# Attention phase of a decoder layer: the key scores of every unit alternate with the projections

## The chip, the core and the metric

One core of a Trainium2 chip runs the whole program. It has five engines that work side by side, each through its own queue in order: TensorE (PE, matrix products; its loading of weights is shown as PEld), VectorE (DVE), ScalarE (ACT), GpSimd (POOL) and SyncE (SP), which issues the transfers. Engines wait for each other by semaphores only, so an instruction that waits also holds up everything behind it on its own engine. The metric is the time of one execution on the device in microseconds (us); lower is better.

## What is computed

Three sublayers follow each other over x of shape 8 x 512 x 512, each with a residual sum and a layer norm. Only the first, the self-attention, is touched by the change. Cut to what matters:

```python
kv = _ln(x, kvn_w, kvn_b) @ kv_w + kv_b            # 8 x 512 x 1024
q  = _ln(x, qn_w, qn_b) @ q_w + q_b
q, k = _rotary(q, ...), _rotary(k, ...)            # 16 heads of 32
qn, kn = _ln(q, ln_w, ln_b), _ln(k, ln_w, ln_b)    # over a head's 32
scores = einsum('bhqd,bhkd->bhqk', qn, kn) / sqrt(32)
attn = softmax(scores, axis=-1)
a = einsum('bhqk,bhkd->bhqd', attn, v)
x = _layernorm(x + (a @ out_w + out_b))            # then retention and the coupling network
```

## The kernel before, in words

The attention works in **units**: one batch entry b of 8 and one group g of four heads (G = 4, HG = 4), so 32 units, U = 4 b + g. A matrix with 512 rows has four tiles of 128 (T = K = 4), so a unit has T x HG = 16 score tiles of 128 x 512. Each engine's function `unit` goes through 16 **steps** i = 0 to 15, and tables at the head of the file say how many items of each kind have been issued by the end of a step; `within(DONE, i)` gives those that belong to step i. Three units are under way at once on PE. In unit U it issues

- the **query scores** of unit U + 1 (`query_scores`, product at L912, table QS_DONE: none in steps 0 and 1, then one or two a step until step 13). They only serve the softmax: DVE takes the maximum of each row (`row_max`, L527), ACT exponentiates and sums in place (`sum_exps`, L776, one step later). They go through three PSUM banks, so query score m waits for the sum of m - 3.
- the **key scores** of unit U (`key_scores`, L932, table KS_DONE), the same scores with keys on the partitions and the maximum taken off. ACT turns each into probabilities (`exps`, L797). They go through two banks: key score m waits for the exponential of m - 2.
- the **projections** for unit U + 3 (`project_item`, table PROJECT_DONE, sixteen items, each of the three products L887, L888 and L889; four items make one tile of q, k and v), which DVE saves (`save_qkv`, L490 and L492, SAVE_AFTER). Items of the third and fourth tile wait until an earlier tile is saved; with g = 0 there is one bank for them, and each new tile waits for the last one.
- the **weighing** (`weigh`, L942, table WEIGH_AT): four times a unit, the probabilities of one tile of keys times v, for all four heads. It waits for the exponentials of its tile; the exponentials of the tile after the next wait for it, since there are two sets of `probs`.
- two turns of normalised heads (`turn_item`, L898, TURN_AT), the turned inverses of the sums (`spread_inverse`, L950, step 11) and the turned maxima (`transpose_max`, L919, step 14).

Between two units lies one chain: all row maxima, `transpose_max` on PE, `save_max` on ACT (L789, two copies), `spread_max` on DVE (L533). Key scores 0 and 1 wait for one copy each, key score 2 for `spread_max`. The text below calls the start of `save_max` **S**; the time from one S to the next is the length of a unit. At the start of a unit DVE runs `spread_max`, `normalise` (L551) of the unit before, `head_mean`, two `save_qkv`, then from step 2 on row maxima; ACT runs its exponentials of step 0, then `attn_hi` (L803), which waits for `normalise`, and at steps 1 and 2 a `square` each (L760). POOL runs per unit `centre`, `head_norm` (L369 is a slow power) and `rotate`, and in units with g >= 2 `add_bias` (L383); `head_norm` waits for `head_var` on DVE (L508, L511, steps 2 and 3).

Units with g = 0 have more: the output product of the batch before (OUT_DONE, L955 to L957), and from step 12 on the turned input of the next batch (`z_item`, L880, then `z_high` on ACT, L754, and `z_low` on DVE, L482). In the last three units (b = 7, g > 0) no projections are left; the last one has output products instead (OUT_PART_AT).

Only the order inside each queue is written by hand; the changed lines are in the tables and in the two `unit` functions of ACT and PE. In the kernel before, units with g = 0 and with g > 0 have tables of their own, and with g > 0, as in step 0 of every unit, all projections of a step stand ahead of all its key scores.

Of the kernel before, what the change touches and what calls it, by code (L numbers as in the profile page):

```python
# [20 lines left out]
T = S // P  # L21
# [3 lines left out]
HG = H // G  # L25
GQ = HG * HD
EPS = 1e-5

KS_DONE = ((2, 5, 7, 8, 9, 10, 11, 12, 13, 14, 15, 16, 16, 16, 16, 16),
           tuple(min(4 * (i + 1) // 3, T * HG) for i in range(16)))  # L30
QS_DONE = tuple(min(max(4 * (i - 1) // 3, 0), T * HG) for i in range(16))
PROJECT_DONE = (4, 8, 9, 10, 12, 14, 15, 16, 16, 16, 16, 16, 16, 16, 16, 16)
WEIGH_AT = ((3, 5, 9, 13), (5, 7, 10, 13))
TURN_AT, SAVE_AFTER = ((8, 11), (8, 10)), ((0, 1, 4, 7), (0, 1, 4, 7))
OUT_DONE, ADD_AFTER = (0, 0, 1, 3, 4, 6, 8, 10, 12, 14, 16, 16, 16, 16, 16, 16), (4, 6, 8, 10)
Z_AT, Z_HIGH_AT, Z_LOW_AFTER = (12, 12, 13, 13), (12, 13, 13, 14), (12, 13, 13, 14)
# [50 lines left out]
def within(done, i):  # L87

    return range(done[i - 1] if i else 0, done[i])
# [48 lines left out]
def attention_phase(nc, x, x1, w, ctx_in, w_next, ret):  # L138
# [6 lines left out]
    with ctx:  # L145
# [595 lines left out]
        def _(act):  # L741
# [68 lines left out]
            def unit(b, g, left, more):  # L810
                U = G * b + g
                for i in range(T * HG):
                    if left == 0 and i in SPLIT_AT:
                        next_higher(*SPLITS[SPLIT_AT.index(i)])
                    if left >= 1 and i >= 1:
                        for m in within(QS_DONE, i - 1):
                            sum_exps(U + 1, (g + 1) % 2, m)
                    for m in within(KS_DONE[g > 0], i):
                        exps(U, m)
                    if i == ATTN_HIGH_AT and counts(U):  # L820
                        attn_hi(U - 1, (g - 1) % G)
                    if i == INVERSE_SAVE_AT:
                        save_inverse(U)
                    for s in range(2):
                        if left >= 2 and i == SQUARE_AT[s]:
                            square(U + 2, s)
                        if left >= 2 and i == TURN_HIGH_AT[g > 0][s]:
                            turn_high(U + 2, s, bank_t[s])
                    for t in range(T):
                        if g == 0 and left == 4 and i == X_NORM_AT[t]:  # L830
                            x_norm(b + 1, t)
                        if g == 0 and left == 4 and i == Z_HIGH_AT[t]:
                            z_high(b + 1, t)
                    if i == SAVE_MAX_AT and left >= 1:
                        save_max(U + 1, (g + 1) % 2)
# [37 lines left out]
        def _(pe):  # L873
# [139 lines left out]
            def unit(b, g, left, more):  # L1013
                U = G * b + g
                for i in range(T * HG):
# [1 line left out]
                        for m in within(QS_DONE, i):  # L1017
                            query_scores(U + 1, (g + 1) % 2, m)
                    items = list(within(PROJECT_DONE, i)) if left >= 3 else []
                    keys = list(within(KS_DONE[g > 0], i))  # L1020
                    if g > 0 or i == 0:
                        for m in items:
                            project_item(b, g, m)
                        for m in keys:
                            key_scores(U, g % 2, m)
                    else:
                        for n_item in range(max(len(items), len(keys))):
                            if n_item < len(keys):
                                key_scores(U, g % 2, keys[n_item])
                            if n_item < len(items):  # L1030
                                project_item(b, g, items[n_item])
                    if i in WEIGH_AT[g > 0]:
                        weigh(U, g, WEIGH_AT[g > 0].index(i))
                    if left == 0 and OUT_PART_AT <= i < OUT_PART_AT + T * (G - 1):
                        if i == OUT_PART_AT:
                            pe.wait_ge(attnT_done, U)
# [1161 lines left out]
```

## Time and profile before

| what | value |
|---|---|
| median of three runs | 2010.94 us (2009.02 to 2013.51) |
| the profiled execution | 2008.56 us |
| its span in the trace | 2006.8 us |
| attention units, S of the first to S of the last | 86.15 to 1044.09 us |
| PE busy, share of the span | 88% |
| DVE | 73% |
| ACT | 63% |
| POOL | 43% |
| granted TensorE clock, mean | 0.954 of 2.4 GHz |

The busy shares are averages over three phases. The attention takes the first half of the span, and only there does POOL have much to do. A matmul's end is modelled, so neighbouring matmuls overlap in the rows: the pace of a stretch is read from the starts. The clock is given as a share of 2.4 GHz: 1.00 is that level, 0.50 is 1.2 GHz, and a value between them is a mixture over time.

### The profile page before, as it was taken

How to read it: one execution, taken by the hardware profiler on the slowest of the kernel's cores; microseconds unless marked ns; L12 is line 12 of the kernel's file. 1: busy time of each engine (PE TensorE's matmuls, PEld its weight loads, DVE VectorE, ACT ScalarE, POOL GpSimd, SP SyncE). 2: the span in 40 equal slices, each digit the busy share in tenths (PEclk: the TensorE clock that was granted, in tenths of full speed). 3: DMA queues.
4: the chain of work that ended last, by engine and by line, in shares of the span. 5: the costliest groups of instructions: out<-in, count | busy, mean ns of one | idle time of the engine just before them, and what ended most of it. 6: DMA issues, size and time to landing. Idle time of an engine off the chain costs nothing. (4 is left out here: it accounts for less than half of the span.)

```text
span 2006.8 us, 26502 instructions
## 1 busy us (share of the span) xinstructions
PE 1763.3 (88%) x8648; PEld 1322.4 (66%) x8648; DVE 1467.1 (73%) x2915; ACT 1263.7 (63%) x2674; POOL 866.4 (43%) x802
## 2 busy tenths in 40 slices
PE   6788898888898898888888999999998999999972
PEld 5556665656566565665536888888886777777751
DVE  7678687786777867777664777777764688888875
ACT  3388787887878868788683232322224667777764
POOL 3678678686876868768621222222220000000000
PEclk9799999999999999999978999999998999999986
DMA  4222132322323223222252111111121011111111
GB/s 154 54 84 64 54 105 64 100 59 67 93 63 107 52 67 97 59 86 55 72 167 111 63 39 47 53 53 63 63 89 56 10 42 64 64 64 64 42 42 63
DMA packets 86184, 141.06 MB, mean 70 GB/s; under 512 B 16544, under 2 KB 19616, under 8 KB 86048
## 3 DMA queue, kind: packets, MB, share of 16 engines
q1 hardware_dynamic: 86048, 139.37, 22.9%
q8 instruction: 70, 1.15, 0.2%
q14 instruction: 66, 0.54, 0.1%
HBM read 63.82 MB, written 25.17 MB: 44 GB/s over the span
## 5 line engine op out<-in xcount | busy, mean ns | idle before, releaser
L527 DVE TENSOR_REDUCE a_neg_max<-a_max 128x1 fp32r<-128x512 f32 x512 | 340.5, 685 | 151.5 <-PE a_max L912 150.4
L797 ACT ACTIVATE a_probs<-a_exp 128x512 f32<-128x512 f32 x512 | 297.3, 607 | 172.2 <-PE a_exp L932 172.0
L776 ACT ACTIVATE a_max<-a_max,a_neg_max 128x512 f32<-128x512 f32 x512 | 346.1, 687 | 17.5 <-DVE a_neg_max L527 16.7
L912 PE MATMUL a_max<-a_stack 96*128 96x512 f32 x512 | 220.5, 457 | 86.1 <-ACT a_max L776 77.9
L369 POOL TENSOR_TENSOR a_rstd<-a_rstd,a_minus_half 128x16 f32<-128x16 f32 x64 | 185.9, 2905 | 81.6 <-DVE a_rstd L511 81.5
L1728 POOL TENSOR_TENSOR f_yrstd<-f_yrstd,f_minus_half 128x4 f32<-128x4 f32 x8 | 11.0, 1374 | 473.4 <-DVE f_yrstd L1747 473.4
L912 PEld LDWEIGHTS a_max<-a_stack 96*128 96x128 f32 x512 | 98.9, 196 | 176.1 <-ACT a_max L776 128.9
L932 PE MATMUL a_exp<-a_stack 100*128 100x512 f32 x512 | 195.9, 416 | 12.2 <-ACT a_probs L797 9.0
L887 PE MATMUL a_t<-a_w_hi,a_zT_hi 128*128 128x384 f32 x500 | 179.6, 359 | 18.6 <-DVE a_v L492 15.6
L888 PE MATMUL a_t<-a_w_lo,a_zT_hi 128*128 128x384 f32 x500 | 172.3, 345 | 0.0
L889 PE MATMUL a_t<-a_w_hi,a_zT_lo 128*128 128x384 f32 x500 | 171.8, 344 | 0.0
L942 PE MATMUL a_o<-a_probs,a_v 128*32 128x512 f32 x1024 | 146.1, 644 | 0.0
L932 PEld LDWEIGHTS a_exp<-a_stack 100*128 100x128 f32 x512 | 100.4, 197 | 33.9 <-ACT a_probs L797 13.2
L2021 PE MATMUL f_l<-f_h_hi,f_w_hi 128*128 128x512 f32 x240 | 100.3, 418 | 23.9 <-DVE f_h_lo L1737 23.3
L1453 ACT ACTIVATE r_kq_hi<-r_part 128x512 fp32r<-128x512 f32 x64 | 37.0, 625 | 133.8 <-POOL r_part L1320 133.8
L887 PEld LDWEIGHTS a_t<-a_w_hi,a_zT_hi 128*128 128x128 f32 x500 | 97.8, 196 | 33.5 <-DVE a_v L492 23.8
L776 ACT ACTIVATION_READ_ACCUMULATOR a_max<-a_max,a_neg_max 128x1 f32 x512 | 118.9, 232 | 0.0
L2021 PE MATMUL f_w<-f_xT_hi,f_w_hi 128*128 128x512 f32 x256 | 106.1, 414 | 7.4 <-DVE f_xT_lo L1737 7.4
L363 POOL TENSOR_TENSOR a_n<-a_n,a_mean 128x512 f32<-128x512 f32 x64 | 72.8, 1141 | 76.1 <-DVE a_mean L500 75.3
L888 PEld LDWEIGHTS a_t<-a_w_lo,a_zT_hi 128*128 128x128 f32 x500 | 97.9, 196 | 8.7
L2022 PE MATMUL f_w<-f_xT_hi,f_w_lo 128*128 128x512 f32 x256 | 102.0, 398 | 0.0
L2023 PE MATMUL f_w<-f_xT_lo,f_w_hi 128*128 128x512 f32 x256 | 101.9, 398 | 0.0
(282 smaller groups left out, 4812.0 us busy)
## 6 DMA issues: line engine op xcount, KB each, us to landing
a_stack<-a_nT_hi SPq DMA_DIRECT2D x512, 64.0 KB, 2.0
a_stack<-a_nT_lo SPq DMA_DIRECT2D x256, 64.0 KB, 2.0
a_z<-x SPq DMA_DIRECT2D x8, 1024.0 KB, 7.9
a_y<-x SPq DMA_DIRECT2D x8, 1024.0 KB, 5.6
r_xn<-x SPq DMA_DIRECT2D x8, 1024.0 KB, 5.7
r_cn<-ctx SPq DMA_DIRECT2D x8, 1024.0 KB, 7.9
x<-r_xn SPq DMA_DIRECT2D x16, 512.0 KB, 2.8
f_xn<-x SPq DMA_DIRECT2D x8, 1024.0 KB, 5.6
```

The costliest lines, as they stand in the source:

```text
L369: nc.gpsimd.tensor_tensor(rstd[:, c], rstd[:, c], minus_half[:, :], ALU.pow).then_inc(pool_step, 1)
L527: nc.vector.tensor_reduce(neg_max[:, t, ROW + h:ROW + h + 1].bitcast(F32R), bank_max[i % NB][:, :], AX_X, ALU.max, negate=True).then_inc(m ...
L776: nc.scalar.activation(bank_max[i % NB][:, :], bank_max[i % NB][:, :], ACT.Exp, bias=neg_max[:, t, ROW + h:ROW + h + 1], accum_out=sums[:, ...
L797: nc.scalar.activation(probs[:, kt % 2, h, :], bank_exp[i % 2][:, :], ACT.Exp).then_inc(exp_done, 1)
L887: mm(bank, zT_hi[:, k, at], w_hi[:, k, g, :], start=k == 0, stop=False)
L888: mm(bank, zT_hi[:, k, at], w_lo[:, k, g, :], start=False, stop=False)
L889: last = mm(bank, zT_lo[:, k, at], w_hi[:, k, g, :], start=False, stop=k == K - 1)
L912: mm(bank_max[i % NB][:, :], stack[0:ROW, par, h, t * P:(t + 1) * P], stack[0:ROW, par, HG + h, :], start=True, stop=True).then_inc(score_ ...
L932: mm(bank_exp[i % 2][:, :], stack[0:ROW + HG, par, HG + h, kt * P:(kt + 1) * P], stack[0:ROW + HG, par, h, :], start=True, stop=True).then ...
L942: last = mm(bank_o[at, :], v[:, g, kt, at], probs[:, kt % 2, h, :], start=kt == 0, stop=kt == T - 1, tile_position=(0, h * HD))
L2021: mm(bank, a_hi, b_hi, start=first, stop=False)
L2022: mm(bank, a_lo, b_hi, start=False, stop=False)
```

## The change

One table of key scores and one of weighings now hold for every unit. In a step of PE, key scores and projections alternate, a key score first; in step 0 two projections stand ahead. Nothing is added or removed in number.

- KS_DONE: with g > 0 it was 1, 2, 4, 5, 6, 8, 9, 10, 12, 13, 14, 16 by the end of steps 0 to 11; with g = 0 it was 2, 5, 7, 8, 9 and so on to 16 at step 11. It is now 2, 5, 7, 9, 10 and so on to 16 at step 10. ACT's exponentials follow the same table.
- WEIGH_AT: steps 5, 7, 10, 13 (g > 0) and 3, 5, 9, 13 (g = 0) become 3, 5, 8, 12.
- Order on PE within a step, after the query scores and ahead of the weighing: alternating everywhere.

```diff
-KS_DONE = ((2, 5, 7, 8, 9, 10, 11, 12, 13, 14, 15, 16, 16, 16, 16, 16),
-           tuple(min(4 * (i + 1) // 3, T * HG) for i in range(16)))
+KS_DONE = (2, 5, 7, 9, 10, 11, 12, 13, 14, 15, 16, 16, 16, 16, 16, 16)
 QS_DONE = tuple(min(max(4 * (i - 1) // 3, 0), T * HG) for i in range(16))
 PROJECT_DONE = (4, 8, 9, 10, 12, 14, 15, 16, 16, 16, 16, 16, 16, 16, 16, 16)
-WEIGH_AT = ((3, 5, 9, 13), (5, 7, 10, 13))
+WEIGH_AT = (3, 5, 8, 12)
...
-                    for m in within(KS_DONE[g > 0], i):
+                    for m in within(KS_DONE, i):
                         exps(U, m)
...
                     items = list(within(PROJECT_DONE, i)) if left >= 3 else []
-                    keys = list(within(KS_DONE[g > 0], i))
-                    if g > 0 or i == 0:
-                        for m in items:
-                            project_item(b, g, m)
-                        for m in keys:
-                            key_scores(U, g % 2, m)
-                    else:
-                        for n_item in range(max(len(items), len(keys))):
-                            if n_item < len(keys):
-                                key_scores(U, g % 2, keys[n_item])
-                            if n_item < len(items):
-                                project_item(b, g, items[n_item])
-                    if i in WEIGH_AT[g > 0]:
-                        weigh(U, g, WEIGH_AT[g > 0].index(i))
+                    keys = list(within(KS_DONE, i))
+                    ahead = 2 if i == 0 else 0
+                    for m in items[:ahead]:
+                        project_item(b, g, m)
+                    for n_item in range(max(len(items) - ahead, len(keys))):
+                        if n_item < len(keys):
+                            key_scores(U, g % 2, keys[n_item])
+                        if n_item + ahead < len(items):
+                            project_item(b, g, items[n_item + ahead])
+                    if i in WEIGH_AT:
+                        weigh(U, g, WEIGH_AT.index(i))
```

## Rows read from the trace of the kernel before

**Rows 1.** Busy time by stage: stretch, length, then PE, PEld, DVE, ACT, POOL, clock, DMA.

```profile
86.15:1044.09 957.94, 839.98 (x4320) 576.52 (x4318) 695.78 (x1385) 760.27 (x1789) 693.97 (x636) 0.96 0.29 78
```

**Rows 2.** The same view, single units from S to S: g = 0, 1, 2, 3, 2.

```profile
332.41:373.40 40.99, 36.52 (x193) 26.74 (x192) 23.65 (x46) 29.11 (x64) 26.25 (x26) 1.00 0.22 63
373.40:400.56 27.16, 23.88 (x131) 16.41 (x130) 21.87 (x42) 23.33 (x57) 21.85 (x21) 1.00 0.47 138
400.56:428.05 27.49, 23.40 (x130) 16.22 (x129) 23.33 (x46) 23.20 (x56) 22.15 (x21) 1.00 0.24 59
428.05:455.04 26.99, 23.84 (x130) 16.05 (x129) 24.89 (x56) 23.33 (x57) 22.77 (x20) 1.00 0.24 59
...
523.60:552.88 29.28, 25.64 (x132) 17.51 (x132) 23.39 (x46) 23.32 (x57) 22.79 (x22) 0.93 0.21 51
```

**Rows 3.** Waits, 86.15 to 1044.09 us: who waited for whom, us, times, longest.

```profile
ACT a_probs L797 <- PE a_exp L932: 167.6, 185, 4.8
...
PE a_max L912 <- ACT a_max L776: 72.8, 72, 1.7
```

**Rows 4.** Timeline of ACT at the start of unit g = 2: start, duration, instruction, [idle before].

```profile
402.57 0.60 ACT L797 ACTIVATE a_probs<-a_exp 128x512 f32<-128x512 f32 x1 [0.94 <-PE a_exp L932]
...
404.85 0.60 ACT L797 ACTIVATE a_probs<-a_exp 128x512 f32<-128x512 f32 x1 [1.19 <-PE a_exp L932]
...
405.87 1.07 ACT L797 ACTIVATE a_probs<-a_exp 128x512 f32<-128x512 f32 x2
...
407.34 0.67 ACT L776 ACTIVATE a_max<-a_max,a_neg_max 128x512 f32<-128x512 f32 x1
```

**Rows 5.** Timeline of PE in the same unit.

```profile
402.08 0.39 PE L932 MATMUL a_exp<-a_stack 100*128 100x512 f32 x1
...
404.42 0.39 PE L932 MATMUL a_exp<-a_stack 100*128 100x512 f32 x1
...
405.41 0.63 PE L932 MATMUL a_exp<-a_stack 100*128 100x512 f32 x2
...
411.68 1.06 PE L942 MATMUL a_o<-a_probs,a_v 128*32 128x512 f32 x8
```

**Rows 6.** Timeline of DVE in the same unit.

```profile
401.18 0.81 DVE L533 CAST a_stack<-a_stack 4x1024 fp32r<-4x1024 f32 x1 [0.87 <-ACT a_stack L789]
402.02 0.70 DVE L551 TENSOR_TENSOR a_o<-a_o,a_inverse 128x512 f32<-128x512 f32 x1
...
405.22 0.68 DVE L527 TENSOR_REDUCE a_neg_max<-a_max 128x1 fp32r<-128x512 f32 x1
...
418.44 1.89 DVE L527 TENSOR_REDUCE a_neg_max<-a_max 128x1 fp32r<-128x512 f32 x3
```

**Rows 7.** Timeline of POOL in the same unit.

```profile
407.05 2.91 POOL L369 TENSOR_TENSOR a_rstd<-a_rstd,a_minus_half 128x16 f32<-128x16 f32 x1 [2.26 <-DVE a_rstd L511]
...
427.33 2.54 POOL L383 TENSOR_TENSOR a_y<-a_y,a_out_bias 128x512 f32<-128x512 f32 x2
```

**Rows 8.** Timeline of PE, last query score of the same unit.

```profile
425.59 0.50 PE L912 MATMUL a_max<-a_stack 96*128 96x512 f32 x1 [1.63 <-ACT a_max L776]
```

**Rows 9.** Timelines of PE and DVE, start and end of unit g = 0.

```profile
337.04 0.44 PE L887 MATMUL a_t<-a_w_hi,a_zT_hi 128*128 128x384 f32 x1 [1.38 <-DVE a_v L492]
...
367.27 1.04 PE L880 MATMUL a_exp<-a_ident,a_z 128*128 128x128 f32 x8
...
335.23 0.69 DVE L498 TENSOR_REDUCE a_mean<-a_n 128x16 f32<-128x512 f32 x1 [0.70 <-POOL a_n L355]
...
368.95 0.69 DVE L482 TENSOR_TENSOR a_zT_lo<-a_exp,a_zT_hi 128x512 fp32r<-128x512 f32 x1 [0.79 <-ACT a_zT_hi L754]
```

**Rows 10.** Timeline of PE, unit U = 29 (b = 7, g = 1), no projections left.

```profile
996.77 0.80 PE L912 MATMUL a_max<-a_stack 96*128 96x512 f32 x1 [3.04 <-DMA a_stack<-a_nT_lo]
```

**Rows 11.** Busy time in two stretches that follow each other, unit from 523.60; columns as Rows 1.

```profile
541.00:544.40 3.40, 1.85 (x11) 0.73 (x11) 3.15 (x7) 2.64 (x8) 3.24 (x5) 1.00 0.01 2
544.40:547.80 3.40, 3.40 (x15) 1.68 (x15) 1.19 (x3) 2.71 (x8) 3.32 (x5) 0.52 0.00 0
```

## The prediction, on record before the changed kernel ran

> **What bounds the kernel now.** First the table by stage: the change touches the attention units only, 958 us of the span [rows 1]; the rest keeps its code, and I give it no change. Next the units one by one. A unit with g = 0 takes 41 us and PE shows 36.5 busy: PE sets it. The others take about 27 us, with ACT 23.3 busy, PE 23.4 to 23.9, DVE 21.9, 23.3 and 24.9 for g = 1, 2, 3, POOL around 22 [rows 2]. No engine is full there; they take turns. The waits say who misses whom: ACT waited 167.6 us in all for a key score, the largest entry of any engine there, and PE waited 72.8 us for ACT's sums before a query score [rows 3]. So ACT is starved at one place and late at another.
>
> The timelines of the unit with S = 400.56 show both places. ACT's first exponential starts at 402.57 after 0.94 us idle, the second at 404.85 after 1.19 more, and at the first sum, 407.34 or S + 6.8, four exponentials are done [rows 4]. PE explains it: key score 0 stands behind four projections and key score 1 behind four more, at 402.08 and 404.42 [rows 5]; four items thus cost (2.34 - 0.23) / 4 = 0.53 us each, where 0.23 is the pace of two products of 512 columns (0.63 for two against 0.39 for one). From the first sum on ACT hardly rests, and at the unit's end PE waits 1.63 us for it before the last query score [rows 8]. Work that ACT does in the first 7 us shortens the end, unless DVE or POOL come in between.
>
> **The change, unit by unit.** Nothing is added or removed, so each term is a shift of starts. Steps I use: an exponential every 0.49 us (two in 1.07) [rows 4], a sum every 0.66, a maximum every 0.60 (three in 1.89) [rows 6], a key or query score 0.23, an item 0.53, a weighing 1.0 [rows 5]. From a key score's start to its exponential 0.49 (402.08 to 402.57) [rows 4, 5]. From ACT back to PE I take 0.75, the 0.60 of an exponential and 0.15, a chosen value.
>
> *Front, g > 0.* PE: two items, key 0 at S + 0.75 (the copy of `save_max`), an item, key 1 at S + 1.6, an item, key 2 at S + 2.4; `spread_max` ends at S + 1.4 here [rows 6], so that wait is no obstacle. Then key 3 at 3.1, key 4 at 3.9 to 4.3 since it needs exponential 2, and that one is behind `attn_hi`, which needs `normalise` (402.02 + 0.70 = S + 2.2) [rows 6]. Four items late, step 2 begins at S + 5.2 to 5.7, where it began at S + 4.1: the query scores start **1.1 to 1.6 us later**. That is the price: while PE waits for an exponential, projections and query scores stand behind. ACT reaches the first sum at S + 7.7, 0.9 later than now, with seven exponentials done instead of four (1.47 us). After that, weighing 0 goes ahead of query score 2, and at S + 13 the same five sums are done as now, with eleven exponentials against eight and two weighings against one. So ACT is ahead by 3 x 0.49 = 1.5 us, and up to 2.3 where the 0.4 and 0.7 waits of the middle vanish too.
>
> *End, g = 1.* DVE has 5 us to spare, so ACT sets the end. I carried the sums through: the last ends at S + 25.4, the next S at 25.6, against 27.16 here and some 26.7 in other units of this kind. I take **-1.4**.
>
> *End, g = 2.* `x_stats` stands on DVE at steps 5 and 7. The row maximum of step 8 starts at S + 17.9 now [rows 6]; with query scores later and key scores no help to DVE, I get the same 17.9. ACT, ahead, waits 1.2 us for it, then has 7 sums, 2 exponentials and 3 copies left, 7.7 us: next S at 26.5 against 27.49. **-1.0**.
>
> *End, g = 3.* DVE is busy 24.9 of 27.0 [rows 2]. Its maxima 2 and 3 start 0.7 later than now, and of its later idle time about 1.0 can be squeezed. **-0.3**.
>
> *Weighings.* The last one moves from behind query score 15 into PE's wait of 1.63 us before it [rows 8], which costs nothing with g > 0.
>
> *g = 0.* The front had this order already but for step 0, and its fifth projection waits for DVE's save, behind a `head_mean` that waits for POOL [rows 9]. POOL starts its power at S + 6.5 in unit g = 2 and works without a pause until 429.9 [rows 7]; with the first row maximum later, `head_var` and this power come 0.8 to 1.0 later, while the unit gets shorter. I find POOL's rotations done 0.5 us later relative to the S of g = 0, so PE, which sets this unit, waits 0.4 more: +0.4. At the end, weighing 3 now stands in step 12, ahead of the first `z_item`s at 367.27. They move 1.0 later; `z_high` had about half of that to spare, DVE's `z_low` already waits 0.79 for it [rows 9], and from there DVE sets the end: +0.5. Together **+0.9** in each of eight units.
>
> *Last three units.* In U = 29 PE stood 3.04 us for a transfer before query score 0, with key scores 2 and 3 behind it [rows 10]; the new order puts keys 2 to 4 ahead of it and lets ACT use that wait: -1.8. U = 30 has a shorter wait of the kind: -1.5. In the last unit the weighing is one output item (0.7) sooner: -0.7. Together **-4.0**.
>
> *Clock.* Ten of the 21 units with g > 0 and projections ran partly at the lower level. In one, PE had 1.85 us of work in 3.40 and the clock went from 1.00 to 0.52 in the next stretch [rows 11]; that unit took 29.28, the one like it 27.49, so 1.8 us [rows 2]. By the rows the fall follows PE's thin stretch. The change moves keys and weighings out of steps 8 to 13, so those get thinner: in my working for g = 2 PE has two query scores, a key score and a turn, 1.2 us, between S + 17.4 and S + 21, and no more for g = 3. It also fills the front. Bounds: -18 if all ten go, +20 if all the other eleven units join. I take two more net, nearer the lower change because the existing thin stretch, too, fell in only half the units: **+4**.
>
> Sum: 7 x (-1.4 - 1.0 - 0.3) = -18.9; 8 x 0.9 = +7.2; -4.0; +4: **-11.7 us**. Profiled execution 2008.56 - 11.7 = 1996.9. The median lies 2.4 above that execution, so 1999.2 on its scale: I say **1999**.
>
> The Trainium skill, "TensorE: Matmul & The Clock Gate", Part 1, says that "the default state is throttled, and activity releases the throttle". The trace agrees that the clock falls after PE's thin stretch [rows 11]. The rule speaks against a change that thins the end of each unit. It gives the third rival below, which is worked out from rows.
>
> **Rivals.**
> 1. *All of ACT's wait comes back.* A unit like g = 2 has 3.3 us of it. If DVE and POOL let themselves be pulled forward, 2.3 of it in each of 21 units is 48 us: 1963. For: the waits are the largest entry [rows 3]. Against: DVE's 24.9 of 27 with g = 3, and the query scores get later. Half of it would be 1987.
> 2. *The gain is swallowed*, -1 to -3 us in all, about 2010: DVE and POOL hold g = 2 as well as g = 3 (each loses 0.8 at the front through the first row maximum), and what g = 1 gives is returned in g = 0. Also the case in which key scores ahead do little since PE stands on their exponentials.
> 3. *The clock, and it is slower.* PE's end of a unit gets thin enough that the clock falls in all the units of g = 2 and 3 that escape now, and in some of g = 1: 14 x 1.8 = 25 us instead of 4. Then -15.7 + 25 = +9, about 2020. It decides from nine more lowered units on (15.7 / 1.8). For: half the units do it already, and keys and weighings leave just that place. Against: a slow stretch there falls partly into PE's waiting.
>
> **Chances.** Forecast (1986 to 2006) 0.48; rival 1, 0.14; rival 2 (2007 to 2015) 0.18; rival 3 (above 2015) 0.20. Range: the forecast's own spread, rival 2, half of rival 1 and half of rival 3: 1978 to 2019. Beyond 0.2% (about 4 us, which is what a measurement of this kernel can tell from none): faster 0.62, same 0.18, slower 0.20.
>
> **What will show it.** Right: in a unit with g > 0 the first exponential starts near S + 1.2 and seven are done before the first sum at about S + 7.7; ACT's wait for key scores falls from 167.6 to about 110; PE's wait for sums grows; g = 1 units near 25.6, g = 2 near 26.5, g = 3 within 0.5 of now, g = 0 near 42. Wrong: g = 3 shortened by over 1 us (DVE was not the bound), g = 0 unchanged (POOL and the `z` chain had slack), or many units with g > 0 above 28 us at a clock below 0.96 (rival 3).

## The result, and the profile after

| | before | changed |
|---|---|---|
| median of four runs each, same chip | 2010.6 us | 2030.75 us (2028.56 to 2033.23) |
| ratio to before, 95% interval | | 1.0096 (1.0059 to 1.0133) |
| span of the profiled execution | 2006.8 us | 2026.7 us |
| attention units, S of the first to S of the last | 957.94 us | 978.49 us |
| granted clock, mean | 0.954 | 0.946 |

The change costs 19 us (0.96%) where a gain of 12 was forecast; 2031 also lies outside the forecast's range, which ended at 2019. In the profiled pair the spans differ by 19.9 us and the attention units by 20.6, so the loss lies in them alone. The view of the whole stage of the changed kernel comes first, then four single units: stretch, length, then busy time of PE, PEld, DVE, ACT and POOL, clock, DMA. The units are those of the batch shown in [rows 2], g = 0, 1, 2, 3. All lines of the changed file stand one lower.

```profile
85.93:1064.42 978.49, 858.67 (x4320) 586.67 (x4318) 709.40 (x1385) 773.91 (x1789) 695.00 (x636) 0.94 0.28 77
...
341.66:383.77 42.11, 36.70 (x194) 26.81 (x193) 24.48 (x46) 29.36 (x64) 25.00 (x24) 1.00 0.20 59
383.77:410.28 26.51, 24.17 (x130) 16.47 (x129) 21.56 (x42) 23.65 (x57) 20.58 (x19) 1.00 0.48 141
410.28:438.32 28.04, 24.87 (x130) 17.04 (x129) 23.44 (x46) 23.83 (x56) 23.26 (x23) 0.94 0.23 57
438.32:467.99 29.67, 25.91 (x130) 17.49 (x129) 24.80 (x55) 23.93 (x56) 24.00 (x22) 0.88 0.22 55
```

g = 1 is 0.65 us shorter than in [rows 2], but g = 0 is 1.1, g = 2 is 0.55 and g = 3 is 2.7 us longer, the last two at a lower clock. Over all units, from the lengths S to S of both traces:

| units | before, sum | changed, sum | difference | forecast |
|---|---|---|---|---|
| seven with g = 1 (b = 0 to 6) | 189.9 | 187.0 | -2.9 | -9.8 |
| seven with g = 2 | 195.5 | 194.6 | -0.9 | -7.0 |
| seven with g = 3 | 194.9 | 208.0 | +13.1 | -2.1 |
| eight with g = 0 | 325.6 | 338.0 | +12.4 | +7.2 |
| U = 29 and 30 | 52.0 | 50.8 | -1.2 | -3.3 |

The waits of the same stretch (who waited for whom, us in all, times, longest):

```profile
ACT a_probs L796 <- PE a_exp L931: 123.2, 199, 3.4
ACT a_max L775 <- DVE a_neg_max L526: 52.0, 65, 1.8
PE a_max L911 <- ACT a_max L775: 43.8, 51, 2.0
...
PEld a_max L918 <- DVE a_neg_max L526: 35.0, 24, 1.7
```

Against [rows 3] ACT's wait for key scores fell by a quarter and PE's for sums by more than a third. The second line is the one that grew: ACT waits 52.0 us for row maxima, 23.5 of them in the seven units with g = 3, 15.0 in those with g = 2 and 3.8 in those with g = 1. Before, the same view had

```profile
ACT a_max L776 <- DVE a_neg_max L527: 13.2, 34, 0.8
```

The start of the unit g = 2 (S = 410.28), ACT and POOL, in the form of [rows 4] and [rows 7]:

```profile
411.52 1.30 ACT L796 ACTIVATE a_probs<-a_exp 128x512 f32<-128x512 f32 x2 [0.17 <-PE a_exp L931]
...
413.27 1.08 ACT L796 ACTIVATE a_probs<-a_exp 128x512 f32<-128x512 f32 x2
414.57 0.60 ACT L796 ACTIVATE a_probs<-a_exp 128x512 f32<-128x512 f32 x1 [0.21 <-PE a_exp L931]
...
416.80 0.60 ACT L796 ACTIVATE a_probs<-a_exp 128x512 f32<-128x512 f32 x1 [0.16 <-PE a_exp L931]
...
417.82 0.65 ACT L775 ACTIVATE a_max<-a_max,a_neg_max 128x512 f32<-128x512 f32 x1
```

```profile
417.89 2.91 POOL L368 TENSOR_TENSOR a_rstd<-a_rstd,a_minus_half 128x16 f32<-128x16 f32 x1 [3.09 <-DVE a_rstd L510]
```

The front came as worked out: first exponential at S + 1.24, seven done before the first sum at S + 7.54 (forecast 1.2, seven, 7.7). POOL's power starts at S + 7.6. But then comes DVE's group of three maxima, which [rows 6] has at S + 17.9:

```profile
429.29 1.89 DVE L526 TENSOR_REDUCE a_neg_max<-a_max 128x1 fp32r<-128x512 f32 x3
```

That is S + 19.0, not "the same 17.9". In the unit g = 3 (S = 438.32) the same lateness decides how a unit ends. The lateness is built up earlier. This is the maximum of step 5, of query score 5, in the kernel before (unit from 428.05), then in the changed one:

```profile
441.15 0.69 DVE L527 TENSOR_REDUCE a_neg_max<-a_max 128x1 fp32r<-128x512 f32 x1 [1.07 <-PE a_max L912]
```

```profile
452.05 0.69 DVE L526 TENSOR_REDUCE a_neg_max<-a_max 128x1 fp32r<-128x512 f32 x1 [0.60 <-PE a_max L911]
```

It starts at S + 13.10 before and at S + 13.73 after, 0.63 later. Behind it DVE makes a copy that takes 1.08 us and not 0.43 (the rows stand in the last section), another 0.65. The rest of the unit, first on DVE, then on ACT and PE:

```profile
457.11 1.29 DVE L526 TENSOR_REDUCE a_neg_max<-a_max 128x1 fp32r<-128x512 f32 x2
...
463.39 0.69 DVE L526 TENSOR_REDUCE a_neg_max<-a_max 128x1 fp32r<-128x512 f32 x1 [1.04 <-PE a_max L911]
...
465.80 1.29 DVE L526 TENSOR_REDUCE a_neg_max<-a_max 128x1 fp32r<-128x512 f32 x2 [1.11 <-PE a_max L911]
```

```profile
457.83 0.66 ACT L775 ACTIVATE a_max<-a_max,a_neg_max 128x512 f32<-128x512 f32 x1 [1.25 <-DVE a_neg_max L526]
```

```profile
458.66 0.79 PE L911 MATMUL a_max<-a_stack 96*128 96x512 f32 x1 [1.97 <-ACT a_max L775]
...
463.29 1.94 PE L941 MATMUL a_o<-a_probs,a_v 128*32 128x512 f32 x8
465.15 0.84 PE L911 MATMUL a_max<-a_stack 96*128 96x512 f32 x2
```

Read it as a relay. The pair of maxima with step 8's starts at S + 18.8; before it started at 445.42 in the unit from 428.05, S + 17.4. Of these 1.4 us, 0.63 are the late query scores and 0.65 the longer copy. In g = 2 the split is another: the copy was long before too (1.19 us in the unit from 400.56, 1.29 in the changed one), and the maximum of step 5 is 1.03 later, S + 13.74 for 12.71, so there the late query scores are nearly all of it. In the unit g = 3 shown, ACT waits 1.25 us for the first of the pair and PE 1.97 for ACT's sum. The clock falls, as in [rows 11]:

```profile
457.00:460.40 3.40, 1.74 (x7) 1.41 (x7) 3.16 (x15) 2.57 (x7) 1.43 (x2) 0.73 0.00 0
460.40:463.80 3.40, 2.75 (x12) 1.49 (x14) 2.36 (x5) 3.32 (x9) 3.17 (x6) 0.50 0.00 0
463.80:467.20 3.40, 2.25 (x11) 0.47 (x4) 2.29 (x5) 1.46 (x5) 3.24 (x5) 0.76 0.17 42
```

At that level the last weighing takes 1.94 us, not 1.06, and the last two query scores stand behind it. They start at S + 26.83; before, query score 15 started at S + 24.52.

### The profile page after: what moved, and what is told of

It is laid out like the page before. It is cut to its first block and busy times, and to the rows that moved or that the text cites. A ratio compares the mean times of both kernels' runs of the same rounds, so it can differ in the third digit from the quotient of the medians.

```text
span 2026.7 us, 26502 instructions
## 1 busy us (share of the span) xinstructions
PE 1780.8 (88%) x8648; PEld 1330.1 (66%) x8648; DVE 1480.9 (73%) x2915; ACT 1277.5 (63%) x2674; POOL 866.5 (43%) x802
## 5 line engine op out<-in xcount | busy, mean ns | idle before, releaser
L796 ACT ACTIVATE a_probs<-a_exp 128x512 f32<-128x512 f32 x512 | 303.7, 600 | 140.2 <-PE a_exp L931 128.3
L931 PE MATMUL a_exp<-a_stack 100*128 100x512 f32 x512 | 216.3, 426 | 7.4 <-ACT a_probs L796 3.2
L886 PE MATMUL a_t<-a_w_hi,a_zT_hi 128*128 128x384 f32 x500 | 179.4, 359 | 23.5 <-DVE a_v L491 20.6
L2017 PE MATMUL f_l<-f_h_hi,f_w_hi 128*128 128x512 f32 x240 | 100.4, 418 | 24.8 <-DVE f_h_lo L1733 24.2
L775 ACT ACTIVATION_READ_ACCUMULATOR a_max<-a_max,a_neg_max 128x1 f32 x512 | 112.6, 220 | 0.0
```

Of the source, the lines that this page charges most:

```text
L775: nc.scalar.activation(bank_max[i % NB][:, :], bank_max[i % NB][:, :], ACT.Exp, bias=neg_max[:, t, ROW + h:ROW + h + 1], accum_out=sums[:, ...
L796: nc.scalar.activation(probs[:, kt % 2, h, :], bank_exp[i % 2][:, :], ACT.Exp).then_inc(exp_done, 1)
L886: mm(bank, zT_hi[:, k, at], w_hi[:, k, g, :], start=k == 0, stop=False)
L931: mm(bank_exp[i % 2][:, :], stack[0:ROW + HG, par, HG + h, kt * P:(kt + 1) * P], stack[0:ROW + HG, par, h, :], start=True, stop=True).then ...
L2017: mm(bank, a_hi, b_hi, start=first, stop=False)
```

## The experiments

Fourteen variants, each against the kernel before on the same chip. The last column is (ratio - 1) x the time before beside it, the scale used from here on. What is said of single units comes from one profiled execution of each variant.

| | what | median | before | ratio (95%) | us |
|---|---|---|---|---|---|
| | the change | 2030.8 | 2010.6 | 1.0096 (1.0059-1.0133) | +19 |
| e1 | change, last weighing in step 13 | 2037.4 | 2008.1 | 1.0133 (1.0085-1.0181) | +27 |
| e2 | change, unneeded products in step 10, g >= 2 | 2026.5 | 2008.1 | 1.0080 (1.0053-1.0107) | +16 |
| e3 | change, `x_stats` in g = 1 and 2 | 2069.8 | 2008.1 | 1.0301 (1.0264-1.0338) | +60 |
| e4 | change in g = 1 and b >= 6 only | 2007.9 | 2008.1 | 0.9998 (0.9981-1.0016) | 0 |
| e5 | change, weighings in 4, 6, 8, 12 | 2078.3 | 2012.4 | 1.0326 (1.0307-1.0346) | +66 |
| e6 | both tables, old order | 2045.3 | 2012.4 | 1.0161 (1.0138-1.0184) | +32 |
| e7 | new order, old tables | 2000.0 | 2012.4 | 0.9936 (0.9918-0.9954) | -13 |
| e8 | change in g = 0 only | 2030.4 | 2012.4 | 1.0087 (1.0059-1.0114) | +18 |
| e9 | change in g > 0 only | 2021.2 | 2012.2 | 1.0045 (1.0025-1.0064) | +9 |
| e10 | e7, first keys of g > 0 sooner | 1996.1 | 2012.2 | 0.9922 (0.9901-0.9942) | -16 |
| e11 | e7, unneeded products, g > 0 | 2001.6 | 2012.2 | 0.9948 (0.9924-0.9972) | -10 |
| e12 | e7, new weighings in g > 0 | 2086.6 | 2014.8 | 1.0366 (1.0341-1.0392) | +74 |
| e13 | e7, both tables in g = 0 | 2024.5 | 2014.8 | 1.0053 (1.0035-1.0072) | +11 |
| e14 | e7, new weighings in g = 0 | 2015.7 | 2014.8 | 1.0014 (0.9996-1.0031) | +3 |

### First round: what ends g = 3, and is g = 1 worth anything

**e1**, the changed kernel with the last weighing back in step 13.

```diff
-WEIGH_AT = (3, 5, 8, 12)
+WEIGH_AT = (3, 5, 8, 13)
```

> The changed kernel with one number put back: the fourth weighing in step 13, behind query scores 14 and 15, and not in step 12 ahead of them. Theory A (place of the weighing): in units g = 3 of batches 0 to 5 it lies ahead of the last query scores and takes 1.9 us at the lower clock, and with g = 0 it pushes the first z_items back 1.5 us. Then g = 3 falls from about 30.2 to 28.5, g = 0 from 42.2 to about 41.3, and the total by 15 to 20 us (about 2013). Theory B (DVE and the clock set these units, the place does not matter): g = 3 stays above 29.7, g = 0 gives 0.5 at most, total 2024 to 2030.

Theory A is right on g = 3, which took 28.77 us (median; 30.23 in the changed kernel), so the place of the last weighing is worth 1.5 us there, with what the higher clock (0.94 for 0.89) gave. It is wrong on the total: +27 with an interval that overlaps the change's, so e1 is no faster and not shown to be slower either. In a unit with g = 0 the time from the second turn to the unit's end went back from 8.03 to 7.30 us, the value before, so that term (0.73) is the weighing's. But the unit as a whole took 42.96 (expected 41.3) at a clock of 0.96, g = 1 took 27.77 at 0.93 for 26.52, and g = 2 took 30.19 at 0.84 for 28.11. The local gains were not kept.

**e2**, the changed kernel with eight products of 512 columns that nobody reads, written to a projection bank that is free at the start of step 10, g = 2 and 3, b = 0 to 5.

```diff
+                    if i == FILL_AT and g >= 2 and more and left >= 1:
+                        pe.wait_ge(qkv_saved, T * (U + 3) + 4 if left >= 3 else T * G * B)
+                        for m in range(FILL):
+                            mm(bank_t[1][:, :], stack[0:ROW, (g + 1) % 2, 2, 0:P], stack[0:ROW, (g + 1) % 2, HG + 2, :],
+                               start=True, stop=True)
```

> The changed kernel with eight products of 512 columns more at the start of step 10 in units g = 2 and 3 of batches 0 to 5, written to a bank of PSUM that is free there and whose contents are overwritten by the next turn: work that nobody needs, in the place where PE stands 2 us for a sum. Theory C (the low clock is what costs): the clock stays at 1.00 to the end of the unit, g = 3 falls from 30.2 to 28 or less, the mean clock of these units rises from 0.88 to 0.97 or more, total about 2015 or less. Theory B (DVE chain alone): the clock rises and g = 3 stays within 0.5 of 30.2, total 2027 to 2033. If the extra products themselves delay the query scores, g = 3 grows.

Here is a unit with g = 3, at full clock with the work added, and the longest of the units with g = 0:

```profile
436.29:464.62 28.33, 25.49 (x138) 17.52 (x137) 25.53 (x56) 23.88 (x56) 22.86 (x21) 1.00 0.23 57
464.62:509.70 45.08, 39.47 (x194) 29.31 (x193) 24.38 (x46) 29.47 (x65) 26.60 (x26) 0.92 0.20 58
```

The medians are 28.33 against 30.23, so 1.9 us of a g = 3 unit are the clock's. It is still 1.3 above the 26.99 that [rows 2] shows at full clock, and that is the lateness itself (DVE is busy for 25.5 of it). Theory C is right on the clock and nearly on g = 3 (28 or less), wrong on the total, which was to fall to 2015: units with g = 0 took 42.8 by the median for 42.2, the longest 45.08 at 0.92, so part of the gain was given back there. The total itself (+16) can't be told from the change's +19.

**e3**, the changed kernel with DVE's `x_stats` taken out of g = 3: steps 8 and 11 of g = 1, steps 5 and 7 of g = 2.

```diff
-                    if g >= 2 and more and i in STATS_AFTER:
-                        x_stats(b + 2, 2 * (g - 2) + STATS_AFTER.index(i))
+                    if 1 <= g <= 2 and more and i in STATS_AFTER[g - 1]:
+                        x_stats(b + 2, 2 * (g - 1) + STATS_AFTER[g - 1].index(i))
```

> The changed kernel with the four input statistics (x_stats, 1.3 us each on DVE) in steps 8 and 11 of g = 1 and steps 5 and 7 of g = 2, where they were in steps 5 and 7 of g = 2 and 3; x_final stays in step 9 of g = 3. Theory D (the statistics between the row maxima make the new order late): g = 3 falls from 30.2 towards the 26.6 that the unit U = 27 without statistics takes, 27 to 28, g = 2 stays near 28, g = 1 grows from 26.5 to 27.5 at most; total about 2010 to 2018. If POOL or x_final set g = 3 instead, it stays above 29.5 and the total at 2028 or more.

It is slower by far, against 2010 to 2018 expected, but the loss is in g = 1, where DVE now waits 2.74 us for the transfer of the input. Where g = 3 is left in peace it answers the question (g = 1, then g = 3):

```profile
397.83:429.91 32.08, 26.23 (x131) 18.03 (x131) 24.64 (x48) 23.91 (x57) 22.33 (x21) 0.86 0.38 116
457.97:484.54 26.57, 23.40 (x130) 16.26 (x129) 22.20 (x49) 23.69 (x56) 22.40 (x20) 1.00 0.25 61
```

With DVE at 22.2 us in place of 24.8 and the new tables, g = 3 takes 26.57 at full clock, less than before. In that unit the maximum of step 5 is as late as in the changed kernel (S + 13.66) and the copy behind it as long (1.14), yet the maxima of step 8 start at S + 17.34: without the statistics DVE makes the lateness good. Of the six g = 3 units that had statistics, two did so; in the other four the maxima up to step 8 are over 1 us later from the first query score on, the clock is 0.84 to 0.90, and they took 29.2 to 29.9. The changed kernel itself has a seventh without statistics, U = 27: 26.61 at full clock. So DVE's load between the maxima decides whether late query scores make a unit with g = 3 late.

**e4**, the change only where DVE has room: g = 1 of all batches and g = 2, 3 of b = 6 and 7.

```diff
-                    for m in within(KS_DONE[g > 0], i):
+                    for m in within(KS_DONE[form(g, more)], i):
```

Here `form` is 0 for g = 0, 1 for g >= 2 while `x_stats` are left, else 2, with the new tables and the new order.

> The kernel before with the new tables and the new order only in the units whose DVE has no input statistics and no output product beside them: g = 1 of every batch, and g = 2 and 3 of the last two batches. Theory D expects a gain there and nothing lost elsewhere: g = 1 falls from 27.2 to 26.5, U = 26 from 27.0 to 25.4, U = 27 from 27.5 to 26.6, U = 29 from 28.3 to 26, all others as in the kernel before, total 2000 to 2004. If the lower clock moves to other units or POOL hands the gain back in the next unit, the total stays within 4 us of 2010.6.

There is no difference in the total, where 2000 to 2004 was expected. The changed units mostly gave what they should (g = 1 -0.5 on the average, U = 26 -1.6, U = 27 -0.9, U = 29 -2.5, but U = 30 +2.1). Of the untouched ones, the units with g = 0 took 5.2 us more in all (four of them 42.4 to 42.7) and the six with g = 3 3.6 more (four of them 29.0 to 29.2, at a clock of 0.93 to 0.96), while the six with g = 2 took 4.5 less. In sum most of the gain was taken back.

### Second round: order or tables, g = 0 or the rest

**e5**, the changed kernel with the first two weighings a step later.

```diff
-WEIGH_AT = (3, 5, 8, 12)
+WEIGH_AT = (4, 6, 8, 12)
```

> The changed kernel with the first two weighings one step later, steps 4 and 6 for 3 and 5, so that query scores 2, 3 and 5 stand ahead of them on PE. Theory E (PE hands the query scores over too late: in g = 3 of the changed kernel DVE waited 0.46 us for query score 2 and 0.60 for query score 5, each of which stood behind a weighing of 1.0): the maximum of step 8 in g = 3 starts near S + 17.8 and not at 18.8, PE's wait of 1.97 us after it shrinks below 1.3, g = 3 falls from about 30.2 to 28.5 or less, total 2012 to 2020. Rival (DVE's own work, the key scores and POOL make it late, not the place of the weighing): g = 3 stays above 29.5 and the total within 5 us of 2030.

Both expectations missed: the total is 2078 and g = 3 takes 31.0 us by the median. The idea that a later weighing mends the new key scores fell in this form. Query score 2 does start earlier, at S + 7.6 in four of the six units g = 3, but with the key scores that early, exponential 8 needs the set of `probs` that weighing 0 frees, and ACT stands on it with its sums behind (86 to 1080 us):

```profile
ACT a_probs L796 <- PE a_o L941: 88.3, 30, 3.9
```

In the changed kernel that entry is 7.7 us over all units. So the two tables need each other: early key scores want early weighings.

**e6** has both new tables and the old order, **e7** the new order and the old tables.

```diff
+                    ahead = 2 if i == 0 else 0
+                    for m in items[:ahead]:
+                        project_item(b, g, m)
+                    for n_item in range(max(len(items) - ahead, len(keys))):
...
```

> One part alone: the new tables KS_DONE and WEIGH_AT, but with g > 0 and in step 0 the projections of a step ahead of its key scores, as in the kernel before. Theory E: the tables put keys and weighings ahead of the query scores, the order does not; so g = 3 is as long as in the changed kernel (29.5 to 31) and the exponentials gain less at the front, total 2028 to 2040. If the alternation is what delays DVE (save_qkv 1 waits for items 4 to 7), g = 3 is 28 or less and the total at 2015 or less.

> The other part alone: alternating order and two projections ahead in step 0, with the tables KS_DONE and WEIGH_AT of the kernel before. Theory E: key scores 0 to 3 come sooner, the query scores hardly later, so units with g > 0 are as long as in the kernel before or up to 0.5 us shorter, g = 0 unchanged, total 2000 to 2011. If the alternation costs, total above 2015.

Theory E holds for both: e6 has g = 3 at 30.1 and a total near its range, e7 lies in its range. This parts the change in two: tables +32, order -13, together +19.5, and the change measured +19. By this split the gain comes from alternating and the loss from the tables.

**e8** has the change (order and both tables) in units with g = 0 only, **e9** in units with g > 0 only. The weighings of e8, those of e9 being the other way round:

```diff
-WEIGH_AT = ((3, 5, 9, 13), (5, 7, 10, 13))
+WEIGH_AT = ((3, 5, 8, 12), (5, 7, 10, 13))
```

> The kernel before with the new table, order and weighings in units g = 0 alone. By the traces of the changed kernel g = 0 grows by 1.2 us in each of seven units, 0.7 of it at the end by the fourth weighing ahead of the first z_items: g = 0 near 42.2, the others as before, total 2016 to 2021. If what g = 0 gave up came from the later start of POOL in g = 1 to 3, it stays at 41.0 to 41.5 here, total 2008 to 2013.

Of e8, a g = 1 and a g = 2 unit, whose code is that of [rows 2]:

```profile
386.47:415.24 28.77, 25.63 (x130) 17.38 (x130) 21.80 (x42) 23.15 (x57) 22.75 (x21) 0.92 0.46 132
415.24:444.19 28.95, 25.33 (x132) 17.12 (x131) 22.97 (x46) 23.37 (x57) 22.37 (x21) 0.94 0.21 51
```

They took 27.16 and 27.49 before, at full clock. In the two, PE is busy 1.75 and 1.93 us longer for the same instructions, so the clock took it. g = 0 itself came as expected (42.20 by the median), the total did not (2016 to 2021): of the 21 unchanged units 12 ran below 0.96, and 8 in the kernel before. The clock of a unit also differs in the kernel before, so what a single unit lost can't be laid on the one ahead. The total can: it rose by 18 us, where eight units of 1.2 us more make 10.

> The changed kernel with units g = 0 as in the kernel before: the complement of the run in which g = 0 alone was changed (which took 18 us more than before). If the two parts add up, this one takes 2 us more than before (2012 to 2015 beside a before of 2010 to 2012). If each part costs through the lower clock that it brings on, and the second finds the clock already low, they do not add up: g = 3 still 29.5 or more at a clock below 0.95, this one 2020 to 2028.

e9's g = 3 units are as slow as the changed kernel's (median 30.24), so that loss needs nothing of g = 0, and the total is in the range of the second theory. +18 and +9 don't sum to +19, though the intervals (5, 4 and 7 us to either side) are too wide for this alone. Counted from e7 it is clearer: e9 is 22 us above it and e13 (below) 24, together 46, where the change is 32 above it; the gap is 14, give or take some 10. That the two halves share losses of the clock is the likely reason and is not shown by itself.

**e10**: e7 with the front of the new key table in g > 0, the rest of it and the weighings as before.

```diff
-           tuple(min(4 * (i + 1) // 3, T * HG) for i in range(16)))
+           (2, 4, 5, 6, 7, 8, 9, 10, 12, 13, 14, 16, 16, 16, 16, 16))
```

> The order alone (new alternation in every step, which was 0.64% faster than before), and for g > 0 also the front of the new table: key scores 2, 4, 5, 6 and so on by steps 0 to 3 in place of 1, 2, 4, 5, but from step 4 on, and in the weighings, as before. Theory F (what costs is the later part of the tables, weighing 0 and 1 and key scores 8 to 13 ahead of the query scores and sums of steps 3 to 8; the front gains): g = 1 and 2 fall by 0.5 us or more against the order alone (27.1 and 27.0 to 27.7), g = 3 stays near 27.3, total 1990 to 1998. If key scores ahead at the front cost already, since the sums and query scores stand behind them: g = 3 is 28 or more, total 2010 or more.

It is the fastest of all, 0.8% under the kernel before; that it beats e7 isn't shown (the intervals overlap). The total, g = 1 (26.25 by the median for e7's 27.13) and g = 3 (27.39) came as theory F has them, but g = 2, which was to fall, took 28.98 at a clock of 0.91 for e7's 27.71. Put it beside the changed kernel, both g = 3. PE of e10 (S = 429.13):

```profile
436.29 0.39 PE L912 MATMUL a_max<-a_stack 96*128 96x512 f32 x1
...
440.11 1.07 PE L942 MATMUL a_o<-a_probs,a_v 128*32 128x512 f32 x8
441.10 0.50 PE L912 MATMUL a_max<-a_stack 96*128 96x512 f32 x1
```

PE of the changed kernel (S = 438.32):

```profile
445.95 1.06 PE L941 MATMUL a_o<-a_probs,a_v 128*32 128x512 f32 x8
446.95 0.74 PE L911 MATMUL a_max<-a_stack 96*128 96x512 f32 x2
...
450.45 1.06 PE L941 MATMUL a_o<-a_probs,a_v 128*32 128x512 f32 x8
451.45 0.50 PE L911 MATMUL a_max<-a_stack 96*128 96x512 f32 x1
```

Query score 2 starts at S + 7.16 in e10 and at S + 8.63 behind weighing 0 in the changed kernel. Query score 5 starts at 11.97 behind one weighing and eight key scores, and at 13.13 behind two weighings and eleven key scores. And DVE's maximum of step 8 in e10:

```profile
446.56 0.69 DVE L527 TENSOR_REDUCE a_neg_max<-a_max 128x1 fp32r<-128x512 f32 x1
```

That is S + 17.43, where the kernel before has 17.37 and the changed one 18.79. So the first key scores can go ahead without making the maxima late. What makes them late in the changed kernel is the rest of its two tables: ahead of query score 5 that is one more weighing (1.0 us of PE) and three more key scores (0.7), of which 1.16 us show. The rows don't part the two. The copy differs as well: 0.43 us in this unit of e10, 1.08 in the changed kernel.

**e11**: e7 with unneeded products, eight in step 10 and four in step 13, g > 0 and b < 7.

```diff
+                    if i in FILL_AT and g > 0 and left >= 3:
...
+                        for m in range(FILL[FILL_AT.index(i)]):
...
```

> The order alone, with products that nobody needs where PE waits late in a unit (g > 0, batches 0 to 6): eight of 512 columns at the start of step 10 into a bank that the next turn overwrites, four at the start of step 13 into a free one. Of the units with g > 0 of the order alone, ten of 21 ran at a mean clock of 0.96 or less and took some 0.7 us more. Theory G (the lower clock follows PE's thin stretches there): all of these units run at 1.00, total 1988 to 1996. If the extra products delay the query scores as much as the clock gives back, the clock is 1.00 and the total 1998 or more.

The units it fills run at 1.00 and are 0.1 to 0.9 shorter by the median than e7's (26.83, 26.81, 27.18). The units with g = 0, not filled, went from 41.0 to 42.5 by the median, at 0.96, and the total did not move, so theory G is right on the clock and wrong on the total (1988 to 1996). In this run, holding the clock by unneeded products moved the low stretch on.

### Third round: which table

**e12** is e7 with the new weighings in g > 0, key scores as before.

```diff
-WEIGH_AT = ((3, 5, 9, 13), (5, 7, 10, 13))
+WEIGH_AT = ((3, 5, 9, 13), (3, 5, 8, 12))
```

> The new order (2000.0 alone) with the new weighings in units with g > 0 only; all key scores and g = 0 as before. The units with g > 0 lose 20 us between the new order alone (2000.0) and the new order with both new tables (2021.2). Theory A: the weighings do it, since each stands ahead of a query score sooner and the last one ahead of three: 2013 to 2021 here, and DVE's maximum of step 5 waits for PE as in the changed kernel (from S + 13.7 on). Theory B: the key scores of steps 5 to 10 do it, one more item for ACT ahead of each sum: 1998 to 2004 here. Between 2005 and 2012 both share it.

The result is far beyond both expectations, on A's side: +74. Units with g > 0 take 30.4, 30.5 and 30.1 by the median. But the road is not the one that A names. In the unit g = 3 from 454.31 the maximum of step 5 starts at S + 13.26 (e7 13.13) and those of step 8 at S + 18.06 (e7 17.68), a delay that the copy (0.84 us for 0.43) covers. Then PE stands in front of its own weighings, here in the unit from 423.85:

```profile
442.15 1.83 PE L942 MATMUL a_o<-a_probs,a_v 128*32 128x512 f32 x8 [2.44 <-ACT a_probs L797]
...
450.57 1.07 PE L942 MATMUL a_o<-a_probs,a_v 128*32 128x512 f32 x8 [1.09 <-ACT a_probs L797]
```

From 86 to 1040 us PE waited 73.0 us for exponentials there, which the changed kernel does not, since its key scores are ahead too. Early weighings alone cost 87 us over e7; with the early key scores (e9) 22. The key scores pay most of that back, not all. The opposite half, all of the new key table with the old weighings, can't run: key score 10 in step 5 needs exponential 8, which needs weighing 0, behind it on PE. So what the rear half of the key table costs by itself stays open.

**e13** is e7 with both new tables in g = 0, **e14** with the new weighings in g = 0 only.

```diff
-WEIGH_AT = ((3, 5, 9, 13), (5, 7, 10, 13))
+WEIGH_AT = ((3, 5, 8, 12), (5, 7, 10, 13))
```

> The new order with both new tables in units with g = 0 only, g > 0 keeps its tables. If a unit with g = 0 costs 1.2 us more by itself and nothing elsewhere: 2000.0 + 9.6 = 2009.6, units with g > 0 near 27.1, 27.7 and 27.3 as with the order alone. Rival: the changed g = 0 also lowers the clock of the units behind it, as it did with the old order (28.8 and 28.95 with g = 1 and 2): then 2014 to 2020.

> As e13, but only the weighings of g = 0 are new (steps 3, 5, 8, 12), its key scores old. If the last weighing ahead of the first turned inputs costs the 0.7 us read at the end of these units: 2000.0 + 8 x 0.7 = 2005.6, and g = 0 near 41.7. Rival, the key score moved up from step 3 on delays PE's projections or queries instead: within 3 us of 2000.0, g = 0 near 41.0.

Both totals lie above what was expected, 2024.5 for at most 2020 and 2015.7 for 2005.6. g = 0 took 42.28 and 42.23 by the median (e7 41.02): the weighings make the whole of what this unit loses. But e13 as a whole is 8 us slower than e14 (+11 and +3, twelve runs each, the intervals apart), and the key scores of g = 0 are all that differs. In the two profiled executions the units S to S take the same (968.7 and 968.1), so where these 8 us arise stays open. e14 beside e7 shows the place within a unit, the end of U = 8, PE. First e7 (S = 331.35):

```profile
366.24 1.04 PE L880 MATMUL a_exp<-a_ident,a_z 128*128 128x128 f32 x8
367.03 0.72 PE L912 MATMUL a_max<-a_stack 96*128 96x512 f32 x2
367.67 1.07 PE L942 MATMUL a_o<-a_probs,a_v 128*32 128x512 f32 x8
```

and e14 (S = 334.92):

```profile
370.14 1.06 PE L942 MATMUL a_o<-a_probs,a_v 128*32 128x512 f32 x8
371.13 1.09 PE L880 MATMUL a_exp<-a_ident,a_z 128*128 128x128 f32 x8
371.98 0.71 PE L912 MATMUL a_max<-a_stack 96*128 96x512 f32 x2
```

Up to S + 25.2 the two traces agree within 0.04 us. Then the third weighing, now ahead of a query score, makes it 0.8 late, of which 0.25 are left at S + 31; and the fourth moves the last two query scores from S + 35.68 to 37.06. The unit ends 0.97 later. By the medians e14 is 16 us above e7. In the profiled pair the units S to S take 18 us more: 10.0 in the eight with g = 0 and 7.9 in the unchanged ones with g > 0, of which 14 (e7: 9) show a clock under 0.96.

## Why the prediction was wrong

- **Front: right.** First exponential, seven before the first sum, the first sum's time, query scores 1.0 us later (forecast 1.1 to 1.6), ACT's key-score wait from 167.6 to 123.2 (about 110).
- **"I get the same 17.9" (g = 2) and -0.3 (g = 3): wrong, and this is the step that failed.** The forecast let DVE catch up by step 8, and it did not: 19.0 in g = 2, 18.8 for 17.4 in g = 3. The 1.0 us that "can be squeezed" was not there; the `x_stats` between the maxima hold it (e3: 26.57 without them). -0.3 was +1.9 on the average of seven.
- **"Weighing 0 goes ahead of query score 2"** stands in the forecast only as a fact about ACT's lead. By the tables with g > 0, 11 of the 16 query scores (2 to 7, 9 to 11, 14 and 15) have one weighing more ahead of them than before, 1.0 us of PE each time, and up to four key scores more. The forecast priced them as work moved, not as work put ahead of the query scores. In g = 3 it also had no term for DVE's copy, which went from 0.43 to 1.08 us.
- **g = 1, -1.4: right sign, half the size** (-0.65 by the median), and by the sum only -0.4 each. ACT's wait for row maxima is not the reason, with 3.8 us in all seven of these units. What holds them back wasn't found.
- **The last weighing "costs nothing with g > 0": wrong in g = 3.** The clock has fallen by then and the weighing takes 1.94; put back in step 13 (e1), it leaves 28.77 for 30.23, though the total did not gain.
- **PE's wait for sums "grows": wrong.** It fell from 72.8 to 43.8. That PE reached the query scores later itself would explain it.
- **g = 0, +0.9: nearly right in size, half right in cause.** It is +1.2 by the median and +1.55 on the average. The end chain (+0.5) measured 0.73, by weighing 4. The POOL term (+0.4) is not there: in e9, with only the units g > 0 changed, g = 0 takes 40.97 (before 41.00), and in e14, with only its weighings changed, the rest (0.25) is the third weighing.
- **Last three units, -4.0:** U = 29 gave -2.3 (forecast -1.8), but U = 30 +1.2 (forecast -1.5), and from the last S to the end of the span -0.4 (forecast -0.7).
- **Clock, +4: mis-sized.** From before to after, lowered units (under 0.96) with g > 0 went from 8 to 12 of 21 (the forecast's ten include those at 0.96), but each lost more: the g = 3 ones stand at 0.88, not 0.93. By e2 (28.33 at full clock) that is 1.9 us in each of six g = 3 units, 11 us. In the rows it follows the DVE lateness: the clock falls where PE stands for the late sum. The Trainium skill, "TensorE: Matmul & The Clock Gate", Part 1, says activity releases the throttle; the rows agree (full clock with the unneeded products), and e11 shows that for the whole it gave no measurable gain (2001.6 us for e7's 2000.0).

Rival 3 gave the sign (2020 forecast, 2031 measured) with half the mechanism: it had the clock as the only loss, where in g = 3 late maxima go before it. Rival 2 came nearest to those, since it had DVE hold g = 2 and g = 3.

What is shown: the split of order and tables (e6, e7); that the weighings alone cost much in g > 0 with the old key scores (e12) and make the whole loss of a g = 0 unit (e14); that the new tables make the maxima late and the first key scores alone do not (e10); that without DVE's statistics late query scores do no harm in g = 3 (e3), and that the clock adds 1.9 us to such a unit (e2). What is argued only: how e9's 22 us over e7 divide between weighings and later key scores, since e12 loses in another way. The clock's part differs between units with the same code, so no run gives it as a number of its own. One rival was never tested: DVE's long copy. 22 of 31 units have it in the changed kernel, 11 before, 2 in e7 and none in e10. It is 0.65 of the 1.4 us in g = 3, and whether it is a cause of its own or only follows from the shifted times no run tells.

## What to carry over

When an item is moved ahead in an in-order queue, price it on what stood there before: here one weighing of 1 us, and some key scores, came ahead of most query scores, whose consumers (DVE's maxima) had no slack until the unit's end. Split a change that has an order and a table before believing its sum: the order alone gave -0.6% and with the sooner first key scores -0.8%, the tables took 1.6% the other way. And where the clock follows how full PE is, a loss can show in units whose code is untouched, so the parts need not add up.

## What the runs showed of the hardware

- A unit with unchanged code took 28.8 us at a granted clock of 0.92 instead of 27.2 at 1.00, with only units of another kind changed (e8). A weighing takes 1.06 us at 1.00 and 1.94 at 0.50.
- DVE's plain copy of 128 x 512 values took 0.43 us before and 1.08 in the changed kernel (units from 428.05 and 438.32). A POOL operation of the same size ran beside it in both. In the second it had started before the copy, in the first 0.15 us after the copy's start. Over the attention of all sixteen traces, 272 copies began while no such POOL operation was running and took 0.43 to 0.47 us; 224 began inside one, and 213 of them took 0.67 to 1.53.

```profile
442.03 0.43 DVE L544 COPY a_inverses<-a_sums 128x512 f32<-128x512 f32 x1
```

```profile
442.18 1.19 POOL L371 TENSOR_TENSOR a_n<-a_n,a_rstd 128x512 f32<-128x512 f32 x1
```

```profile
452.94 1.08 DVE L543 COPY a_inverses<-a_sums 128x512 f32<-128x512 f32 x1
```

```profile
452.68 1.05 POOL L370 TENSOR_TENSOR a_n<-a_n,a_rstd 128x512 f32<-128x512 f32 x1
```

No run changed this alone.
